# Second edge loop of a four-layer graph kernel: joining maximum and denominator in PSUM with VectorE and ScalarE instead of TensorE, and 36 instead of 32 of 125 gathered columns a turn by TensorE

## The chip, the cores and the metric

One core of one Trainium2 chip runs the whole program. The metric is the time on the device in microseconds (us), the median of several runs. The engines are called TensorE (PE in the profile; PEld are its weight loads), VectorE (DVE), ScalarE (ACT), GpSimd (POOL) and SyncE (SP).

## The reference, cut to what matters

Node features x (12,500 nodes of 32 features) go through four layers, each of which adds to x what it makes of `h = relu(layernorm(x))` over 400,000 edges sorted by receiver. The second layer, the one that is changed, is attention over the edges:

```python
scores = jnp.sum(Q[receiver] * K[sender], axis=1) * scale
smax = jax.ops.segment_max(scores, receiver, num_segments=n)
alpha = jnp.exp(scores - smax[receiver])
Z = jax.ops.segment_sum(alpha, receiver, num_segments=n)
alpha = alpha / (Z[receiver] + 1e-06)
out = jax.ops.segment_sum(alpha[:, None] * V[sender], receiver, num_segments=n)
return x + out @ Wo
```

## The kernel before, in words

The edges are cut into 125 chunks (`NCH`) of 4 groups by 800 edges (`CH`), walked in 25 turns (`TURNS`) of 5 chunks (`RING`). There is one edge loop for each layer, and between the loops a short stage over the nodes. In a chunk's tile, `rows`, each of 128 partitions holds 25 edges (columns) of 32 features. A column is filled with the senders' features in one of two ways.

**By GpSimd**: an indirect DMA (L492) fetches the rows of one column from the table in memory; behind each stands a memset of a tile called `pace` (L497), whose end the engine waits for.

**By TensorE**: `gather_tile` multiplies a one-hot matrix with the node table held in SBUF (`h_parts`): 14 matmuls at L690, in the second loop behind one more, L686, that adds a far value to the rows of the wrong blocks. The block's one-hot row `h0_hot` is made by VectorE in `make_h0_hot` (L904), for the next chunk but one, inside `turn_mz`. VectorE then reduces the tile from PSUM into the column (`pick`, L912). `PE_COLS[1]` says how many columns of each of the five chunks go this way: (7, 7, 6, 6, 6), so 32 of 125, 6.4 a chunk. GpSimd does the other 93. In this loop the tiles have two PSUM banks (`TILE_BUFS[1]` is 2), so that a tile is begun only when VectorE has picked the last but one. The one-hot matrices are cast by ScalarE (L546) from tiles that a DMA brings back (L554), four tiles ahead.

**The order by hand in the second loop**: While VectorE works through chunk r (`attend`, then `turn_in` of chunk r+1, then `turn_mz` of chunk r), TensorE makes the tiles of chunk r+1. In `attend` VectorE scans the queries (L1179) and multiplies them with the keys (L1180); it picks tiles 0 and 1; TensorE sums the products over the features into `acc_wide` (L738: the scores); VectorE scans the running maximum (L1187, with L1185 ahead), subtracts it from the scores (L1190) and picks tiles 2 and 3. Meanwhile ScalarE makes from that difference the decay and the weight by two Relus (L626, L627) and two Exps (L629, L631). Then come the scan of the denominator Z (L1195), the product (L1197), the scan of the messages (L1198), a small copy (L1199), the transpose of the messages out (L1201), and the picks from tile 4 on. `turn_in` transposes the next chunk's rows (L1163) and queries (L1165). `turn_mz` makes the block one-hot (L904) and transposes `acc_wide` out (L1210). On TensorE the tiles 0 and 1 come first, then the scores, the other tiles, and at the end of each chunk 12 matmuls (L745), which write into `acc_wide` the new maximum for the lower half of the features and Z for the upper half: the sum of three products with constant 0/1 matrices (`mz_parts`, loaded by SyncE from `c_mz`). TensorE must have the one-hot row of the next chunk before that chunk's tile 0.

Of the kernel before, what the change touches and what calls it, by code (L numbers as in the profile page):

```python
# [38 lines left out]
ALU = mybir.AluOpType  # L39
# [3 lines left out]
P = 128  # L43
# [14 lines left out]

PE_COLS = ((8, 8, 8, 8, 8), (7, 7, 6, 6, 6), (8, 8, 8, 8, 8), (6, 6, 5, 5, 6))
PACE = 288  # L60
# [17 lines left out]
def gnn_kernel(nc, x_in, src_c, src_pe, dst_c, dst_p, dst_blocks, pattern_c, sh_c, wq, wk, wv, wo, w2, w3,  # L78
               c_ones, c_tri, c_group, c_iota, c_half, c_diag, c_sel, c_expand, c_mz, c_coupling, c_target, c_shift, out):
    KT = x_in.shape[1]  # L80
# [30 lines left out]
    with ExitStack() as ctx:  # L111
# [51 lines left out]
        nb_wide = work[:, 12:14, :].rearrange("p a c -> p (a c)")[:, 0:CH + 1]  # L163
        mz_parts = qh[:, 0:3 * P].rearrange("p (a m) -> p a m", m=P)
        h0_width = max(PE_COLS[1]) * P // 2
# [79 lines left out]
        window_loaded, keep_made, keep_stored = sem("window_loaded"), sem("keep_made"), sem("keep_stored")  # L245
        prod_ready, score_ready, z_ready, mz_made, mz_loaded, nb_ready = sem("prod_ready"), sem("score_ready"), sem("z_ready"), sem("mz_made"), sem("mz_loaded"), sem("nb_ready")
        decay_in, decay_ready, p_in, p_ready = sem("decay_in"), sem("decay_ready"), sem("p_in"), sem("p_ready")
# [109 lines left out]
        def _(sp):  # L357
# [40 lines left out]
            for l in range(LAYERS):  # L398
# [6 lines left out]
                if l == 3:  # L405
                    sp.wait_ge(sh_stored, 32 * NCH + START)
                if l == 1:
                    sp.dma_start(mz_parts.rearrange("p a m -> p (a m)"), c_mz).then_inc(mz_loaded, 16)
                with sp.Fori(0, TURNS) as t:
# [105 lines left out]
        def _(act):  # L515
# [100 lines left out]
            with act.Fori(0, TURNS) as t:  # L616
                for r in range(RING):
# [12 lines left out]
                    act.wait_ge(decay_in, n)  # L630
                    nc.scalar.activation(u, u, ACT.Exp, scale=-1.0).then_inc(decay_ready, 1)  # L631
                    cast_next(1, t, r, range(2, PE_MAX))
                    store(1, t, r, attn_chunks, 2 * CH)
# [30 lines left out]
        def _(pe):  # L664
# [64 lines left out]
            gather_first(1)  # L729
            pe.wait_ge(mz_loaded, 16)  # L730
            with pe.Fori(0, TURNS) as t:
                for r in range(RING):
                    for i in tiles(1, r + 1, range(2)):
                        gather_tile(1, t, i, per_turn[1])
                    pe.wait_ge(prod_ready, chunk_no(0, t, r))
                    pe.wait_ge(outs_ready[(r - 1) % RING], use(1, t, 0 if r else -1))
                    for cols in SPANS:
                        last = nc.tensor.matmul(acc_wide[:, cols], group_ones[:, :], prod[:, cols], start=True, stop=True)  # L738
                    last.then_inc(score_ready, 1)
                    for i in tiles(1, r + 1, range(2, PE_MAX)):  # L740
                        gather_tile(1, t, i, per_turn[1])
                    pe.wait_ge(z_ready, chunk_no(0, t, r))
                    for cols in SPANS:
                        for part, rows_in in enumerate((prod, d, Z)):
                            last = nc.tensor.matmul(acc_wide[:, cols], mz_parts[:, part, :], rows_in[:, cols],  # L745
                                                    start=(part == 0), stop=(part == 2))
                    last.then_inc(mz_made, 1)
            for q in range(PIECES):
# [44 lines left out]
        def _(v):  # L793
# [361 lines left out]
            steps1 = steps[0]  # L1155
            per_chunk1 = 5

# [10 lines left out]
            def attend(t, r):  # L1168
# [24 lines left out]
                v.wait_ge(decay_ready, n)  # L1193
                v.wait_ge(p_ready, n)
                nc.vector.tensor_tensor_scan(Z, u, in_ps, last_of(Z), ALU.mult, ALU.add).then_inc(z_ready, 1)  # L1195
                v.wait_ge(z_ready, n)
# [3 lines left out]
                v.wait_ge(outs_stored[r], t * 16 + (1 * TURNS * 16 + START))  # L1200
                then(nc.vector.transpose(row[:, :, 0:D], by_edge(in_ps)))  # L1201
                pick_next(1, t, r, range(4, PE_MAX))
                assert at[0] == per_chunk1

            def turn_mz(t, r):

                make_h0_hot(t, r + 2)
                v.wait_ge(mz_made, chunk_no(0, t, r))
                row = outs[:, r, :].rearrange("p (j f) -> p j f", j=J)
# [214 lines left out]
def constants(KT):  # L1424
# [23 lines left out]
    for k, (n, i) in enumerate(LAYER3_TERMS):  # L1448
# [12 lines left out]
        else:  # L1461
# [18 lines left out]
        "c_expand": (np.arange(mul)[:, None] == inner[None]).astype(np.float32),  # L1480
        "c_mz": np.stack([(group[:, None] == group[None]) & (feature[None] < D // 2),
                          np.eye(P, dtype=bool) & (feature[None] < D // 2),
                          np.eye(P, dtype=bool) & (feature[None] >= D // 2)], axis=1).astype(np.float32).reshape(P, 3 * P),
        "c_coupling": coupling,
# [5 lines left out]
_INS = ("x_in", "src_c", "src_pe", "dst_c", "dst_p", "dst_blocks", "pattern_c", "sh_c", "wq", "wk", "wv", "wo", "w2", "w3",  # L1490
        "c_ones", "c_tri", "c_group", "c_iota", "c_half", "c_diag", "c_sel", "c_expand", "c_mz", "c_coupling", "c_target", "c_shift")

# [46 lines left out]
```

## Time and profile before

| | |
|---|---|
| median of 3 runs | 15984.19 us (15972.8 to 16000.97) |
| profiled execution, first to last instruction (span) | 14816.7 us |
| between that span and the median of the runs | 1167.5 us |
| second edge loop, from its first to its last transposed chunk (L1163) | 3801.3 to 7276.4 us |
| TensorE, VectorE, ScalarE, GpSimd busy over the span | 87%, 65%, 26%, 84% |

The profile gives the span of its execution and no time of its own for what lies around it, so the table sets the span against the median. A row of the timeline gives start, duration, engine, line, operation, output and input, how many instructions were merged, and in brackets how long the engine had been idle and who ended it. A row of groups gives count, busy time, the mean of one, and the idle time ahead. "Clock" is TensorE's granted clock as a share of 2.4 GHz.

### The profile page before, as it was taken

To read this page: it belongs to the slowest core of one execution; us is meant where nothing else is said; L and a number is where in the kernel's file an instruction comes from. 1 tells how busy PE (TensorE), PEld (TensorE's weight loads), DVE (VectorE), ACT (ScalarE), POOL (GpSimd) and SP (SyncE) were. 2 spreads that over 40 slices of the span, in tenths; PEclk is the share of its full clock that TensorE was granted. 3 is DMA by queue.
4 is the path that set the end of the run, shared out by engine and by line. 5 is a ranking of instruction groups with operands and counts; after the bars stand their busy time and mean duration, and the time that the engine had idled before them with its cause. 6 is when DMAs were issued, how large, how long until landed. Compare 5 with 4: busy or idle time off the path is not lost.

```text
span 14816.7 us, 226154 instructions
## 1 busy us (share of the span) xinstructions
PE 12890.3 (87%) x57644; PEld 10677.8 (72%) x57644; DVE 9612.6 (65%) x13223; ACT 3874.6 (26%) x4265; POOL 12431.7 (84%) x18594
## 2 busy tenths in 40 slices
PE   7999999992699999999689999999769999999996
PEld 6888888881577777777578888888756666767764
DVE  7666666664577777777666666666656665666665
ACT  2222222220233333333222222222211111111111
POOL 6888888887888888888778888888888888888884
PEclk9999999995899999999889999999989999999998
DMA  5444444442344444444345555545433333333332
GB/s 174 148 148 157 157 155 151 149 151 46 101 123 122 124 124 123 122 123 124 90 119 130 129 130 128 131 127 131 110 76 87 86 90 83 90 86 87 87 86 56
DMA packets 1340717, 1727.48 MB, mean 117 GB/s; under 512 B 501932, under 2 KB 1145566, under 8 KB 1339646
## 3 DMA queue, kind: packets, MB, share of 16 engines
q10 hardware_dynamic: 705956, 1154.87, 24.6%
q1 hardware_dynamic: 327194, 407.86, 9.6%
q0 software_dynamic: 306880, 158.96, 7.6%
q14 instruction: 668, 5.47, 0.1%
q8 instruction: 19, 0.31, 0.0%
HBM read 1140.23 MB, written 580.36 MB: 116 GB/s over the span
## 4 chain that ended last, share of the span: by engine, by line
POOL 41%; issue 32%; PE 20%; DVE 5%; POOLq 1%; DMA 0%; DVEq 0%; ACT 0%; ACTq 0%; SPq 0%
POOL rows L492 22%; POOL pace L497 16%; PE psum L690 12%; PE psum L773 7%; POOL outs L509 2%; PE psum L764 2%; DVE work L1340 1%; DVE work L1315 1%; POOLq L496 1%; POOL q_edges L471 1%; POOL work L501 1%; DVE tile_rows L924 0%; DVE work L1323 0%; DVE rows L931 0%; DVE outs L1347 0%
## 5 line engine op out<-in xcount | busy, mean ns | idle before, releaser
L690 PE MATMUL psum<-h_parts,one_hot 128*128 128x448 f32 x49406 | 10813.2, 377 | 482.0 <-ACT one_hot L539 262.4
L690 PEld LDWEIGHTS psum<-h_parts,one_hot 128*128 128x128 f32 x49406 | 9428.8, 192 | 1500.6 <-ACT one_hot L539 313.0
L492 POOL DMA_INDIRECT rows<-h_table,idx x9000 | 8662.9, 963 | 1966.9 <-POOL pace L497 1537.1
L546 ACT ACTIVATE one_hot<-keys 128x896 fp32r<-128x896 bf16 x2533 | 2359.9, 950 | 6435.5 <-PE psum L690 4314.0
L497 POOL MEMSET pace<- 128x288 f32 x9000 | 3213.9, 357 | 18.1 <-issue 13.2
L924 DVE TENSOR_TENSOR tile_rows<-psum,h_mask 128x448 f32<-128x448 f32 x2722 | 1686.2, 619 | 1252.3 <-PE psum L690 991.3
L931 DVE TENSOR_REDUCE rows<-tile_rows 128x32 f32<-128x448 f32 x2722 | 1677.0, 616 | 58.9
L773 PE MATMUL psum<-work,bd_t 128*128 128x512 f32 (+1 forms) x3500 | 1359.2, 514 | 240.1 <-DVE work L1323 141.3
L1323 DVE TENSOR_TENSOR work<-psum,work 128x800 f32<-128x800 f32 x875 | 862.7, 988 | 920.9 <-PE psum L764 864.2
L773 PEld LDWEIGHTS psum<-work,bd_t 128*128 128x128 f32 x3500 | 654.9, 193 | 764.4 <-issue 443.4
L912 DVE TENSOR_REDUCE rows<-psum 128x32 f32<-128x448 f32 x807 | 503.1, 623 | 792.0 <-PE psum L690 741.7
L539 ACT ACTIVATE one_hot<-work 128x896 fp32r<-128x896 bf16 x506 | 482.0, 953 | 1493.3 <-DVE work L887 1493.3
L539 ACT ACTIVATE one_hot<-bit_hot 128x896 fp32r<-128x896 bf16 x506 | 482.6, 954 | 883.4 <-DVE bit_hot L887 880.5
L1028 DVE STREAM_TRANSPOSE psum<-rows 128x800 f32<-128x800 f32 x125 | 128.2, 1026 | 864.0 <-DMA rows<-h_table,idx 864.0
L686 PE MATMUL psum<-work 128*128 128x448 bf16 x807 | 296.3, 367 | 308.0 <-DVE work L904 223.6
L745 PE MATMUL psum<-work 128*128 128x512 f32 x1500 | 524.1, 499 | 0.0
L509 POOL DMA_INDIRECT outs<-sums,end_row x294 | 291.6, 992 | 258.3 <-DMA sums<-outs 147.0
L686 PEld LDWEIGHTS psum<-work 128*128 128x128 bf16 x807 | 78.2, 97 | 501.6 <-DVE work L904 276.3
L745 PEld LDWEIGHTS psum<-work 128*128 128x128 f32 x1500 | 284.2, 189 | 210.3 <-issue 179.8
L764 PE MATMUL psum<-work,sel 120*128 120x512 bf16 x1750 | 427.4, 337 | 0.0
L1163 DVE STREAM_TRANSPOSE work<-rows 128x800 f32<-128x800 f32 x125 | 213.7, 1710 | 207.7 <-DMA rows<-h_table,idx 188.4
L1293 DVE STREAM_TRANSPOSE psum<-rows 128x800 f32<-128x800 f32 x125 | 128.2, 1026 | 289.7 <-DMA rows<-h_table,idx 289.7
(202 smaller groups left out, 6198.1 us busy)
## 6 DMA issues: line engine op xcount, KB each, us to landing
keys<-hots ACTq DMA_DIRECT2D x2542, 224.0 KB
keep_in<-keep_flat SPq DMA_DIRECT2D x2000, 100.0 KB
sums<-outs ACTq DMA_DIRECT2D x375, 400.0 KB
rows<-h_table,idx POOLq DMA_INDIRECT x9000
hots<-bit_hot ACTq DMA_DIRECT2D x506, 224.0 KB
hots<-work ACTq DMA_DIRECT2D x506, 224.0 KB
attn<-outs ACTq DMA_DIRECT2D x125, 800.0 KB
edge_in<-pattern_c SPq DMA_DIRECT2D x125, 400.0 KB
```

Of the source, the lines that this page charges most:

```text
L492: nc.gpsimd.indirect_dma_start(out=rows[:, r, j * D:(j + 1) * D], out_offset=None, in_=h_table[:, :], in_offset=bass.IndirectOffsetOnAxis( ...
L497: nc.gpsimd.memset(pace[:, :], 0.0).then_inc(pause_ended, 1)
L509: nc.gpsimd.indirect_dma_start(out=node_rows[:, k * width:(k + 1) * width], out_offset=None, in_=table[:, :], in_offset=bass.IndirectOffse ...
L539: nc.scalar.activation(one_hots[i % LOOK[l]][:, :, :], bit_hots[i % BIT_BUFS[l]], ACT.Copy).then_inc(one_hot_cast, 1)
L546: nc.scalar.activation(one_hots[i % LOOK[l]][:, :, :], loaded_hots[i % BIT_BUFS[l]], ACT.Copy).then_inc(one_hot_cast, 1)
L690: last = nc.tensor.matmul(banks[TILE_BANKS[l][b]][:, 0:H0 * D], one_hots[hot][:, h1, :], h_parts[:, part, h1 * H0 * D:(h1 + 1) * H0 * D], ...
L745: last = nc.tensor.matmul(acc_wide[:, cols], mz_parts[:, part, :], rows_in[:, cols], start=(part == 0), stop=(part == 2))
L764: last = nc.tensor.matmul(bcast[n % 2][:, cols], sel[0:SH_ROWS, n, :], shT[r][:, cols], start=True, stop=True)
L773: last = nc.tensor.matmul(acc_wide[:, cols], bd_t[:, n, :], weighted[n % 4][:, cols], start=(n == 0), stop=(n == PRODUCTS - 1))
L924: nc.vector.tensor_tensor(tile_rows[:, :].rearrange("p (f h) -> p f h", f=D), banks[TILE_BANKS[l][b]][:, 0:H0 * D].rearrange("p (f h) -> p ...
L931: nc.vector.reduce_sum(rows[:, chunk % RING, j * D:(j + 1) * D], tile_rows[:, :].rearrange("p (f h) -> p f h", f=D), axis=AX_X).then_inc(p ...
L1323: nc.vector.tensor_tensor(weighted[n % 4], bcast[n % 2], hT, ALU.mult).then_inc(weighted_ready, 1)
```

## The change

Two things change in the second edge loop. First, the 12 matmuls at the end of a chunk go, with their constant and its load. In their place VectorE makes, ahead of the scan of Z, `max(acc_wide, 0) + mx` in place (the difference to the old maximum, cut at zero, plus the old maximum); ScalarE multiplies it with a 0/1 mask for the lower half of the features, behind its two Exps; and after the transpose of the messages VectorE adds Z times the mask for the upper half. Second, the columns by TensorE become (7, 7, 7, 7, 8), 36 of 125, which leaves 89 to GpSimd.

```diff
-PE_COLS = ((8, 8, 8, 8, 8), (7, 7, 6, 6, 6), (8, 8, 8, 8, 8), (6, 6, 5, 5, 6))
+PE_COLS = ((8, 8, 8, 8, 8), (7, 7, 7, 7, 8), (8, 8, 8, 8, 8), (6, 6, 5, 5, 6))
...
-        mz_parts = qh[:, 0:3 * P].rearrange("p (a m) -> p a m", m=P)
...
-                if l == 1:
-                    sp.dma_start(mz_parts.rearrange("p a m -> p (a m)"), c_mz).then_inc(mz_loaded, 16)
...
                     nc.scalar.activation(u, u, ACT.Exp, scale=-1.0).then_inc(decay_ready, 1)
+                    act.wait_ge(m_made, n)
+                    nc.scalar.activation(acc_wide, acc_wide, ACT.Copy, scale=half[:, 0:1]).then_inc(m_masked, 1)
                     cast_next(1, t, r, range(2, PE_MAX))
...
             gather_first(1)
-            pe.wait_ge(mz_loaded, 16)
...
                     for i in tiles(1, r + 1, range(2, PE_MAX)):
                         gather_tile(1, t, i, per_turn[1])
-                    pe.wait_ge(z_ready, chunk_no(0, t, r))
-                    for cols in SPANS:
-                        for part, rows_in in enumerate((prod, d, Z)):
-                            last = nc.tensor.matmul(acc_wide[:, cols], mz_parts[:, part, :], rows_in[:, cols],
-                                                    start=(part == 0), stop=(part == 2))
-                    last.then_inc(mz_made, 1)
...
-            per_chunk1 = 5
+            per_chunk1 = 6
...
                 v.wait_ge(p_ready, n)
+                nc.vector.scalar_tensor_tensor(out=acc_wide, in0=acc_wide, scalar=0.0, in1=mx[:, 0:CH],
+                                               op0=ALU.max, op1=ALU.add).then_inc(m_made, 1)
                 nc.vector.tensor_tensor_scan(Z, u, in_ps, last_of(Z), ALU.mult, ALU.add).then_inc(z_ready, 1)
...
                 then(nc.vector.transpose(row[:, :, 0:D], by_edge(in_ps)))
+                v.wait_ge(m_masked, n)
+                then(nc.vector.scalar_tensor_tensor(out=acc_wide, in0=Z, scalar=half[:, 1:2], in1=acc_wide,
+                                                    op0=ALU.mult, op1=ALU.add))
                 pick_next(1, t, r, range(4, PE_MAX))
...
                 make_h0_hot(t, r + 2)
-                v.wait_ge(mz_made, chunk_no(0, t, r))
```

The input `c_mz` goes from the argument list and from `constants`.

## Rows read from the trace of the kernel before

**Rows 1.** Stretches: second loop, one turn; length, PE PEld DVE ACT POOL, clock, DMA, GB/s.

```profile
3801.30:7307.00 3505.70, 3195.92 (x13960) 2553.84 (x13961) 2475.95 (x2548) 1252.48 (x1446) 3015.30 (x4614) 0.98 0.43 122
5503.00:5643.10 140.10, 128.76 (x561) 102.71 (x561) 98.98 (x103) 50.25 (x59) 121.60 (x187) 0.98 0.44 123
```

**Rows 2.** The chain of waits, 5500 to 5560 us, shares by line.

```profile
by line: issue 42.0%; POOL rows L492 32.8%; POOL pace L497 24.8%; POOLq L496 1.1%; POOLq L490 0.1%; POOLq L495 0.1%
```

**Rows 3.** Groups on GpSimd, second loop.

```profile
L492 POOL DMA_INDIRECT rows<-h_table,idx x2307 | 2194.6, 951 | 457.7 <-POOL pace L497 399.2 <-issue 58.5
L497 POOL MEMSET pace<- 128x288 f32 x2307 | 828.0, 359 | 1.2
```

**Rows 4.** Line L1163 over the run, and its entry among the loop's waits.

```profile
L1163 DVE STREAM_TRANSPOSE work<-rows x125: 1661/1712/1770, 3801.3 to 7276.4; 128x800 f32<-128x800 f32 x125
DVE work L1163 <- DMA rows<-h_table,idx: 188.4, 61, 112.0
```

**Rows 5.** Timeline of VectorE from 5495 us.

```profile
5495.97 1.88 DVE L1187 TENSOR_TENSOR_SCAN mx<-psum,mx,work 128x800 f32<-128x800 f32 x1 [0.28 <-PE psum L738]
...
5502.02 0.62 DVE L912 TENSOR_REDUCE rows<-psum 128x32 f32<-128x448 f32 x1 [2.45 <-PE psum L690]
5502.87 1.88 DVE L1195 TENSOR_TENSOR_SCAN work<-work,psum 128x800 f32<-128x800 f32 x1 [0.23 <-DVE rows L912]
...
5508.98 0.62 DVE L912 TENSOR_REDUCE rows<-psum 128x32 f32<-128x448 f32 x1
...
5513.03 0.62 DVE L912 TENSOR_REDUCE rows<-psum 128x32 f32<-128x448 f32 x1 [2.57 <-PE psum L690]
...
5516.78 0.41 DVE L904 TENSOR_SCALAR work<-work,half 14x768 bf16<-14x768 int16 x1 [0.15 <-DVE psum L1165]
...
5524.95 1.88 DVE L1187 TENSOR_TENSOR_SCAN mx<-psum,mx,work 128x800 f32<-128x800 f32 x1 [0.29 <-PE psum L738]
...
5552.26 1.88 DVE L1187 TENSOR_TENSOR_SCAN mx<-psum,mx,work 128x800 f32<-128x800 f32 x1 [0.29 <-PE psum L738]
...
5577.90 1.88 DVE L1187 TENSOR_TENSOR_SCAN mx<-psum,mx,work 128x800 f32<-128x800 f32 x1 [0.29 <-PE psum L738]
```

**Rows 6.** Timeline of TensorE over the end of the same chunk.

```profile
5509.76 0.35 PE L686 MATMUL psum<-work 128*128 128x448 bf16 x1 [1.70 <-DVE rows L912]
5509.78 3.21 PE L690 MATMUL psum<-h_parts,one_hot 128*128 128x448 f32 x14
5512.83 4.20 PE L745 MATMUL psum<-work 128*128 128x512 f32 x12
5517.24 0.36 PE L686 MATMUL psum<-work 128*128 128x448 bf16 x1 [0.21 <-DVE work L904]
```

**Rows 7.** Groups of VectorE and ScalarE: the nearest kin of the new instructions.

```profile
L1197 DVE TENSOR_TENSOR psum<-psum,work 128x800 f32<-128x800 f32 x125 | 124.9, 999 | 4.3
L844 DVE SCALAR_TENSOR_TENSOR work<-work,ln 128x448 f32<-128x448 f32 x28 | 17.5, 625 | 0.9
L836 DVE TENSOR_TENSOR work<-xs,ln 128x448 f32<-128x448 f32 x7 | 4.4, 624 | 0.2
L626 ACT ACTIVATE work<-psum 128x800 f32<-128x800 f32 x125 | 104.8, 839 | 535.7 <-DVE psum L1190 535.7
```

**Rows 8.** TensorE's tiles behind long pauses: first, one exception, last of thirteen.

```profile
4728.43 0.55 PE L686 MATMUL psum<-work 128*128 128x448 bf16 x1 [3.71 <-DVE work L904]
4728.48 4.74 PE L690 MATMUL psum<-h_parts,one_hot 128*128 128x448 f32 x14
...
7000.22 3.20 PE L690 MATMUL psum<-h_parts,one_hot 128*128 128x448 f32 x14
...
7279.59 5.67 PE L690 MATMUL psum<-h_parts,one_hot 128*128 128x448 f32 x14
```

**Rows 9.** Windows inside a tile behind a 4.81 us pause, and inside a usual tile.

```profile
5317.60:5319.60 2.00, 2.00 (x6) 1.79 (x7) 1.97 (x2) 0.11 (x1) 1.83 (x4) 0.50 0.18 59
5502.00:5504.80 2.80, 2.80 (x15) 2.46 (x14) 2.52 (x3) 1.69 (x3) 2.47 (x5) 1.00 0.52 133
```

More of the change, by code:

```diff
@@ L78, in gnn_kernel @@
 def gnn_kernel(nc, x_in, src_c, src_pe, dst_c, dst_p, dst_blocks, pattern_c, sh_c, wq, wk, wv, wo, w2, w3,
-               c_ones, c_tri, c_group, c_iota, c_half, c_diag, c_sel, c_expand, c_mz, c_coupling, c_target, c_shift, out):
+               c_ones, c_tri, c_group, c_iota, c_half, c_diag, c_sel, c_expand, c_coupling, c_target, c_shift, out):
     KT = x_in.shape[1]
@@ L245, in gnn_kernel @@
         window_loaded, keep_made, keep_stored = sem("window_loaded"), sem("keep_made"), sem("keep_stored")
-        prod_ready, score_ready, z_ready, mz_made, mz_loaded, nb_ready = sem("prod_ready"), sem("score_ready"), sem("z_ready"), sem("mz_made"), sem("mz_loaded"), sem("nb_ready")
+        prod_ready, score_ready, z_ready, m_made, m_masked, nb_ready = sem("prod_ready"), sem("score_ready"), sem("z_ready"), sem("m_made"), sem("m_masked"), sem("nb_ready")
         decay_in, decay_ready, p_in, p_ready = sem("decay_in"), sem("decay_ready"), sem("p_in"), sem("p_ready")
@@ L1480, in constants @@
         "c_expand": (np.arange(mul)[:, None] == inner[None]).astype(np.float32),
-        "c_mz": np.stack([(group[:, None] == group[None]) & (feature[None] < D // 2),
-                          np.eye(P, dtype=bool) & (feature[None] < D // 2),
-                          np.eye(P, dtype=bool) & (feature[None] >= D // 2)], axis=1).astype(np.float32).reshape(P, 3 * P),
         "c_coupling": coupling,
@@ L1490 @@
 _INS = ("x_in", "src_c", "src_pe", "dst_c", "dst_p", "dst_blocks", "pattern_c", "sh_c", "wq", "wk", "wv", "wo", "w2", "w3",
-        "c_ones", "c_tri", "c_group", "c_iota", "c_half", "c_diag", "c_sel", "c_expand", "c_mz", "c_coupling", "c_target", "c_shift")
+        "c_ones", "c_tri", "c_group", "c_iota", "c_half", "c_diag", "c_sel", "c_expand", "c_coupling", "c_target", "c_shift")
 def laid_out(a):
```

## The prediction

> **What bounds the kernel now.** The change touches one loop of four, so I read in this order: the stretch of that loop, its chain of waits, the groups of the engine that the chain names, and then the timelines of VectorE and TensorE over one chunk.
>
> The stretches [rows 1] show TensorE busy for 128.8 of the 140.1 us of a turn, GpSimd for 121.6, VectorE for 99.0, ScalarE for 50.3. TensorE looks like the bound. The chain of waits says otherwise [rows 2]: it is GpSimd's gathers, its pace memsets and its own issue, nothing else. A column costs GpSimd the gather's 0.951 us, the memset's 0.359 and idle time between them of 457.7/2307 = 0.198 with what stands at the start of a chunk [rows 3]: 1.508 us in all, and 93 x 1.508 = 140.2 us is the turn. The loop's chunks are (7276.4 - 3801.3)/124 = 28.02 us apart [rows 4], 140.1 a turn, 3,503 us for 125.
>
> How far is the second chain behind? VectorE waited 188.4 us for gathered rows, 112.0 of them once, before the first chunk [rows 4]. That leaves 76.4 us over 124 chunks, 0.6 a chunk. So the chain of VectorE and TensorE is only about 3 us a turn shorter than GpSimd's, and whatever lengthens it by more decides. I therefore follow it step by step.
>
> In the timeline of VectorE [rows 5] the maximum scan (L1187) of one chunk stands at 5495.97 and the next at 5524.95: 28.98 us for a chunk in which TensorE makes seven tiles and no gathered row is late. From 5552.26 to 5577.90, with six tiles, it is 25.64. The order inside: pick of tile 3 at 5502.02, scan of Z, product, scan, transpose, pick of tile 4 at 5508.98, of tile 6 at 5513.03, block one-hot at 5516.78, the next maximum. In the timeline of TensorE [rows 6] tile 6 starts at 5509.76, after a pause of 1.70 us that ends with the pick of tile 4: there are two banks, and tile 6 needs tile 4's. The 12 matmuls take 4.20 us at 5512.83, and the next tile 0 starts at 5517.24, after 0.21 us, when the one-hot row is made. So those 12 matmuls lie inside the time in which TensorE has to wait for VectorE's L904 in any case. That is the main reading.
>
> **The change, part by part.**
>
> *The 12 matmuls go.* TensorE is free 4.2 us earlier and then waits for L904: nothing is gained on the chain. In a six-tile chunk it is the same. Their constant's load happens once, beside other work: 0.
>
> *Two sums on VectorE.* Each is 128x800 in fp32 with one input in PSUM. A tensor-tensor of that size and kind takes 0.999 us (L1197); at 128x448 the same operation as the new one takes 0.625 against 0.624 of a tensor-tensor [rows 7]. So 1.0 each, 1.03 with the step's wait. Bounds: 0.6 each (the 448-wide row), and the 1.88 of a scan [rows 5], which also does two operations per element; the equal 448-wide rows speak for 1.0. Both stand on VectorE between the pick of tile 3 and that of tile 4, behind which are queued the remaining picks, the transposes and L904, and TensorE waits for pick 4 and for L904. So all of it is on the chain: +2.06 us a chunk.
>
> *The mask on ScalarE*: an Activate of 128x800 from PSUM, 0.84 us (L626) [rows 7]. It starts behind the first sum and must be done at the second; between them lie the scan of Z, the product, the scan, the copy and the transpose, 5508.98 - 5502.87 = 6.1 us [rows 5]. Hidden. It holds back the one-hot casts behind it on ScalarE by up to 2 us; these run four tiles ahead, and tile 6 is wanted only after pick 4, some 9 us after pick 3. Cost 0; without that cover it would be 0.84 + 1.0. Between 0 and 1 us a chunk, I take 0.
>
> *Columns.* GpSimd: 89 x 1.508 = 134.2 us a turn, 5.9 less. TensorE and VectorE: four chunks of 7 tiles and one of 8. An eighth tile follows the seventh at once (its bank is free), so it adds one tile: 5512.83 - 5509.76 = 3.07 us [rows 6].
>
> *The chain at full clock*: 4 x (28.98 + 2.06) + (28.98 + 2.06 + 3.07) = 124.2 + 34.1 = 158.3 us a turn, against GpSimd's 134.2. The bound moves, and the turn grows by 18.2 us. GpSimd will run ahead and stand idle at `rows_used`.
>
> *TensorE's pauses.* They grow: before tile 6 from 1.70 to 1.70 + 2.06 = 3.8 us, before the next tile 0 from 0.21 to 5517.24 - 5509.78 - 3.21 = 4.25 us [rows 6]. What does such a pause do? In the loop before there are thirteen pauses of 3.6 to 4.8 us ahead of a tile, from 4728.4 to 7279.6 us [rows 8]. Behind one (at 7000.2, pause 3.77) the tile takes the usual 3.23 us; behind the other twelve it takes 4.4 to 5.7, mean of all thirteen 4.80. The stretch inside such a tile shows a granted clock of 0.50, that is 1.2 GHz, against 1.00, 2.4 GHz, in a usual one [rows 9]. Pauses such as the one of 1.70 us [rows 6], some sixty of 1.6 to 1.8, never did this; those of 2.3 to 3.1 did in about half the cases. So each pause costs 4.80 - 3.23 = 1.57 us, and both kinds lie on the chain: VectorE waits for tile 6 and, for the scores, for tiles 0 and 1. Ten pauses a turn: +15.7 us. Bounds: 0, and 2.4 (the longest tile, from 4.16 us) each, 24.
>
> The Trainium skill has this as a rule, page "TensorE: Matmul & The Clock Gate", section "HAM oscillation — how this bites in real kernels": a kernel whose bursts of matmuls are parted by waits loses the full clock in each wait and starts each burst cold. By that rule all ten pauses would cost, with no exception like the one at 7000.2; the trace agrees in twelve of thirteen.
>
> *Sum*: 158.3 + 15.7 = 174.0 us a turn, x 25 = 4,350, against 3,503: +847 us. On the execution shown the span goes from 14,816.7 to 15,664. I take the 1,167.5 us between span and median as unchanged and get 15,984 + 847 = 16,831. The other three loops have the same instructions.
>
> **The rivals.**
>
> *Full clock in most pauses.* For it: the exception at 7000.2, and that the clock was mixed behind pauses not much shorter. Against: twelve of thirteen. 158.3 x 25 = 3,958, +455 us: 16,439.
>
> *GpSimd stays the bound, the kernel gets faster.* The mechanism: VectorE's sums and picks fit into its present waits for tiles (it is busy only 99 of 140 us), so the turn is GpSimd's 134.2 us: -147 us, 15,837. It decides where the other chain is under 134.2 a turn, 26.8 a chunk. For it: TensorE has 12 x 0.35 = 4.2 us a chunk less and one tile in 1.25 chunks more, 2.5 us. Against: the 28.98 us of a seven-tile chunk before, which has no wait for rows in it and whose order is not changed. If some reordering gained just the difference, it would be no change; I see none.
>
> *The clock stays low for longer.* With two colder tiles a chunk TensorE is busy for some 27 of 35 us instead of 25.7 of 28. If tiles 1 and 2 and the scores were slow too, with about 1.5 us more for each of two of them on the chain: 125 x 3 = +375 on top, 17,206. The rows show the second tile at full speed after each such pause, so this is unlikely.
>
> *The change doesn't do what it says* (the columns not moved, the sums alone): then turns of 3 x (25.64 + 2.06) + 2 x 31.04 = 145.2, plus seven or eight pauses of 1.57, 157: +420 us, 16,400. The `PE_COLS` line is plain, so I count this with the first rival.
>
> **How the numbers follow.** Forecast 0.73; full clock in most pauses 0.12; clock low for longer 0.08; GpSimd the bound 0.05; nothing measurable 0.02. The range leaves out the ends: its lower end is half of the pauses at full clock with something to spare (3,958 + 5 x 25 x 1.57 = 4,154, +651, less the sums at 0.6 instead of 1.03, -108: 16,527, I take 16,560), its upper end all ten pauses at 2.0 us (4,458, +955: 16,939), with 50 us for the wider L904 and the mask: 16,990. A measurement of this kernel can tell about 0.2%, 32 us, from no change. Slower 0.93, same 0.02, faster 0.05.
>
> **What would show it right or wrong.** Right: the new sums at 1.0 us each; L1163 every 34 to 35 us; GpSimd no longer gapless, waiting for VectorE; VectorE no longer waiting for DMA at L1163; TensorE with pauses of 3.8 us before tile 6 (released by L912) and 4.2 before tile 0 (released by L904), and tiles of 4.7 us or so behind them; a granted clock near 0.9 in the loop instead of 0.98. Wrong: gathers of GpSimd still gapless; VectorE's seven-tile chunk under 30 us; pauses without the slow tile behind them; a Z scan or second sum that waits for ScalarE.

## The result, and the profile after

| | before | after |
|---|---|---|
| median of the runs compared | 15,989.9 us (4 runs) | 16,517.0 us (4 runs, 16,456.8 to 16,519.8) |
| ratio | | 1.0317, 95% interval 1.0298 to 1.0335 |
| span of the profiled execution | 14,816.7 us | 16,454.3 us |
| second edge loop, first to last chunk | 3,475 us, 28.02 a chunk | 4,472 us, 36.06 a chunk |

The change makes the kernel slower by 527 us. The forecast was 847 us, and the measured time lies 43 us under the low end of the range.

To read the numbers one must know that the same program did not take the same time in each comparison, that is, in each session in which kernels were timed side by side. The kernel before, unchanged, had these medians: 15,990 us in the first comparison (the one of the table), 14,809 in the second, 16,204 in the third, 15,276 in the fourth and 16,028 in the fifth. Within one comparison most of its executions lie within 0.6% of the median. The results carry a chip number: 10 for the second comparison, 14 for the third, 15 for the fourth and 10 again for the fifth; the first has none. So the chip's number does not explain the difference: 14,809 and 16,028 us both stand beside number 10. The text speaks of the conditions of a comparison, and means no more by it than this time of the kernel before. A few single executions took far longer at a much lower granted clock (19,577 us at 0.62 in one case, against 15,281) and are left out of every ratio.

The profile ahead of the prediction has a span of 14,816.7 us, close to the 14,809 of the second comparison, while the runs that it was set against took 15,990. So the two spans and the two second loops in the table must not be compared with each other. The two medians can be.

The page of the kernel after: busy time, then the chain that ended last.

```profile
PE 13401.3 (81%) x57644; PEld 11054.5 (67%) x57644; DVE 9894.6 (60%) x13573; ACT 4089.1 (25%) x4490; POOL 12308.6 (75%) x18394
...
PE 49%; issue 20%; DVE 14%; POOL 11%; another core or an unknown queue 4%; ACT 1%; ACTq 1%; DVEq 0%; POOLq 0%; DMA 0%; SPq 0%
```

GpSimd is no longer most of the chain. The groups of the second loop, kernel after: GpSimd's gathers, the picks, a tile's first matmul, the two sums and the mask.

```profile
L489 POOL DMA_INDIRECT rows<-h_table,idx x2203 | 2100.1, 953 | 1441.0 <-DMA idx<-src_c 1070.8 <-issue 214.7 <-POOL pace L494 155.5
...
L904 DVE TENSOR_REDUCE rows<-psum 128x32 f32<-128x448 f32 x893 | 557.9, 625 | 1524.5 <-PE psum L689 1160.5 <-issue 275.8 <-remote 55.8
L685 PE MATMUL psum<-work 128*128 128x448 bf16 x891 | 367.2, 412 | 1043.3 <-DVE work L896 487.9 <-DVE rows L904 270.7 <-issue 238.4
...
L1197 DVE SCALAR_TENSOR_TENSOR psum<-work,half,psum 128x800 f32<-128x800 f32 x124 | 130.9, 1056 | 4.4
L1187 DVE SCALAR_TENSOR_TENSOR psum<-psum,mx 128x800 f32<-128x800 f32 x124 | 124.0, 1000 | 28.4 <-issue 19.9 <-DVE rows L904 8.5
L630 ACT ACTIVATE psum<-psum,half 128x800 f32<-128x800 f32 x124 | 111.9, 902 | 313.2 <-DVE psum L1187 277.4 <-issue 35.9
```

Against [rows 3], where GpSimd stood idle for 458 us, mostly behind its own pace memset, it now waits 1,071 us for the column indices, which SyncE loads only when VectorE has given the rows' buffer free. TensorE stands idle for 1,043 us ahead of a tile's first matmul: 488 for L896 (the block one-hot, L904 before), 271 for picks (L904, L912 before) and 238 put down to issue, which is time for which the profile shows no cause. The same group in the loop of the kernel before had 304 us:

```profile
L686 PE MATMUL psum<-work 128*128 128x448 bf16 x798 | 292.9, 367 | 303.9 <-DVE work L904 219.4 <-DVE rows L912 83.7
```

The sums take 1.00 and 1.06 us, with no wait ahead of the second. Over the second loop the granted clock is 0.85, against 0.98 in [rows 1] (length, PE PEld DVE ACT POOL, clock, DMA, GB/s):

```profile
3827.00:8299.00 4472.00, 3423.65 (x13871) 2869.74 (x13869) 2751.93 (x2877) 1444.93 (x1662) 2879.69 (x4407) 0.85 0.36 100
```

The timeline of TensorE in the kernel after, one chunk, answers to [rows 6]:

```profile
6057.77 3.19 PE L689 MATMUL psum<-h_parts,one_hot 128*128 128x448 f32 x14
6064.61 0.53 PE L685 MATMUL psum<-work 128*128 128x448 bf16 x1 [3.65 <-DVE rows L904]
6064.63 5.64 PE L689 MATMUL psum<-h_parts,one_hot 128*128 128x448 f32 x14
6074.26 0.56 PE L685 MATMUL psum<-work 128*128 128x448 bf16 x1 [3.99 <-DVE work L896]
6074.31 5.73 PE L689 MATMUL psum<-h_parts,one_hot 128*128 128x448 f32 x14
```

Here is the mechanism that was forecast: a pause of 3.65 us before tile 6 and of 3.99 before the next tile 0, each followed by a tile of 5.6 to 5.8 us instead of 3.2. A tile that is slow in this way, at about half the granted clock, is called cold below.

### The profile page after: what moved, and what is told of

Same layout as the page of the kernel before. It is cut to its first block, busy times and chain, and to the rows that moved or that the text cites. A ratio compares the mean times of both kernels' runs of the same rounds, so it can differ in the third digit from the quotient of the medians.

```text
span 16454.3 us, 227519 instructions
## 1 busy us (share of the span) xinstructions
PE 13401.3 (81%) x57644; PEld 11054.5 (67%) x57644; DVE 9894.6 (60%) x13573; ACT 4089.1 (25%) x4490; POOL 12308.6 (75%) x18394
## 4 chain that ended last, share of the span: by engine, by line
PE 49%; issue 20%; DVE 14%; POOL 11%; another core or an unknown queue 4%; ACT 1%; ACTq 1%; DVEq 0%; POOLq 0%; DMA 0%; SPq 0%
PE psum L689 39%; POOL rows L489 6%; PE psum L765 6%; POOL pace L494 5%; PE psum L756 2%; DVE tile_rows L916 1%; PE psum L685 1%; DVE rows L904 1%; PE psum L736 1%; DVE work L1336 1%; DVE psum L1157 1%; DVE work L1189 1%; ACT one_hot L543 1%; DVE work L1311 1%
## 5 line engine op out<-in xcount | busy, mean ns | idle before, releaser
L689 PE MATMUL psum<-h_parts,one_hot 128*128 128x448 f32 x50806 | 11788.5, 390 | 708.9 <-issue 308.5
L689 PEld LDWEIGHTS psum<-h_parts,one_hot 128*128 128x128 f32 x50806 | 10081.3, 200 | 2011.8 <-issue 838.9
L489 POOL DMA_INDIRECT rows<-h_table,idx x8900 | 8574.8, 963 | 3481.6 <-DMA idx<-src_c 1685.6
L543 ACT ACTIVATE one_hot<-keys 128x896 fp32r<-128x896 bf16 x2633 | 2455.2, 949 | 7764.5 <-PE psum L689 3219.3
L904 DVE TENSOR_REDUCE rows<-psum 128x32 f32<-128x448 f32 x907 | 566.7, 625 | 1648.6 <-PE psum L689 1177.4
L685 PE MATMUL psum<-work 128*128 128x448 bf16 x907 | 374.0, 412 | 1151.0 <-DVE work L896 505.5
L1020 DVE STREAM_TRANSPOSE psum<-rows 128x800 f32<-128x800 f32 x125 | 128.1, 1025 | 619.1 <-DMA rows<-h_table,idx 619.1
L879 DVE TENSOR_TENSOR bit_hot<-keys,target 128x896 bf16<-128x896 int16 x506 | 310.4, 614 | 0.0
L879 DVE TENSOR_TENSOR work<-keys,target 128x896 bf16<-128x896 int16 x506 | 309.6, 612 | 0.0
L756 PEld LDWEIGHTS psum<-work,sel 120*128 120x128 bf16 x1750 | 175.5, 100 | 177.3 <-issue 13.3
L506 POOL DMA_INDIRECT outs<-attn,end_row x98 | 94.6, 966 | 218.2 <-DMA attn<-outs 188.6
```

Of the source, the lines that this page charges most:

```text
L489: nc.gpsimd.indirect_dma_start(out=rows[:, r, j * D:(j + 1) * D], out_offset=None, in_=h_table[:, :], in_offset=bass.IndirectOffsetOnAxis( ...
L543: nc.scalar.activation(one_hots[i % LOOK[l]][:, :, :], loaded_hots[i % BIT_BUFS[l]], ACT.Copy).then_inc(one_hot_cast, 1)
L685: nc.tensor.matmul(banks[TILE_BANKS[l][b]][:, 0:H0 * D], h0_hots[H0_BUF[chunk % RING]][:, q * P:(q + 1) * P], far, start=True, stop=False)
L689: last = nc.tensor.matmul(banks[TILE_BANKS[l][b]][:, 0:H0 * D], one_hots[hot][:, h1, :], h_parts[:, part, h1 * H0 * D:(h1 + 1) * H0 * D], ...
L756: last = nc.tensor.matmul(bcast[n % 2][:, cols], sel[0:SH_ROWS, n, :], shT[r][:, cols], start=True, stop=True)
L904: nc.vector.reduce_max(rows[:, chunk % RING, j * D:(j + 1) * D], banks[TILE_BANKS[l][b]][:, 0:H0 * D].rearrange("p (f h) -> p f h", f=D), ...
```

## The experiments

All times are medians; each ratio is to the kernel before in the same comparison. A loop's length comes from the one profiled execution of a run, and is the time between the first and last of its 125 transposes, so of 124 chunks.

**Second comparison (the kernel before: 14,809 us).** Was the first profile an unusual execution? `e0_before_again` is the kernel before, unchanged.

> The kernel before, unchanged, profiled again. Theory A (the first profiled execution, 14,817 us, was unusually fast; what lay between its span and the median of 15,990 is not fixed time around the program but slower edge loops): span near 15,980, second loop about 32 us a chunk instead of 28.0, loops three and four some 350 and 170 us longer than in that profile, as in the profile of the changed kernel. Rival B (a fixed time around the span): span 14,800 to 14,850, second loop 28.0 us a chunk.

Measured: 14,807.4 us, ratio 0.9999 (0.9990 to 1.0009), span 14,802.2, second loop 28.01. Neither expectation was right as it stood. Span and loop are those of rival B, but its reason falls: the run with that span took 14,804.0 us, so there is no 1,167 us around the span. The first profile is a usual execution under the conditions of the second comparison; what differs are the conditions.

`e1_sums_only` is the changed kernel with the old columns:

```diff
-PE_COLS = ((8, 8, 8, 8, 8), (7, 7, 7, 7, 8), ...
+PE_COLS = ((8, 8, 8, 8, 8), (7, 7, 6, 6, 6), ...
```

> The changed kernel with the old columns (7, 7, 6, 6, 6): only the two sums and the mask. Theory A (VectorE's chain takes the 2.06 us of the sums, and TensorE's longer pauses make the tile behind them cold): three six-tile chunks of 27.7 and two of 31.0, with some eight cold tiles of 1.6 to 2.5 us: 31.5 to 33 us a chunk in the second loop, 16,000 to 16,250 in all if the rest is as in the changed kernel. Rival C (the sums cost nothing, the columns do it): no slower than before, 15,990 or less.

`e2_columns_only` is the kernel before with the new columns, the same line the other way.

> The kernel before with the new columns (7, 7, 7, 7, 8): TensorE keeps the 12 matmuls. Theory A: seven-tile chunks of 29.0 us and one of 32.0, no pause ahead of tile 0 beyond 0.2 us, so hardly a cold tile: 29.5 to 30.5 us a chunk, 16,050 to 16,300 if GpSimd was the bound in the timed runs too, and about 15,700 to 15,990 if those runs' second loop stood at 32 us for another reason. Rival C (columns by TensorE are what costs): 16,400 or more.

Measured: e1 15,083.1 us, ratio 1.0183 (1.0166 to 1.0200); e2 14,829.2, ratio 1.0014 (1.0004 to 1.0024). The transposes of the second loop, e1 and then e2, and those of the fourth loop, e0 and then e2:

```profile
L1157 DVE STREAM_TRANSPOSE psum<-edge_in x125: 1032/1057/1082, 3796.9 to 7697.4; 128x800 f32<-128x800 f32 x125
```

```profile
L1165 DVE STREAM_TRANSPOSE psum<-edge_in x125: 1034/1065/1104, 3798.8 to 7454.2; 128x800 f32<-128x800 f32 x125
L1347 DVE STREAM_TRANSPOSE outs<-work x125: 1667/1732/1799, 11088.1 to 14689.5; 128x800 f32<-128x800 f32 x125
```

```profile
L1347 DVE STREAM_TRANSPOSE outs<-work x125: 1671/1730/1799, 10903.6 to 14663.8; 128x800 f32<-128x800 f32 x125
```

The second loop takes 3,900.5/124 = 31.46 us a chunk with the sums alone and 3,655.4/124 = 29.48 with the columns alone. The prediction's arithmetic gives 157/5 = 31.4 for the first, and 4 x 28.98 + 28.98 + 3.07 = 148.0, so 29.6 a chunk, for the second. Both parts cost, the sums 3.5 us a chunk and the columns 1.5, and rival C falls. Both loops lie a few hundredths of a microsecond under the expected 31.5 to 33 and 29.5 to 30.5. The expected totals (16,000 to 16,250, and 15,700 or more) missed by about 900 us, since they were built on the first comparison's times. Both parts together, the changed kernel itself, were not run in this comparison. But e2 is only 20 us slower in all, though its second loop is 182 us longer: the fourth loop, whose code is the same, takes 3,601 us instead of 3,760. In e1 it takes 3,618.

`e3_early_pick_and_row` does the changed kernel's work in another order on VectorE:

```diff
                 then(nc.vector.tensor_tensor(in_ps, in_ps, hT, ALU.mult))
+                pick_next(1, t, r, range(4, 5))
                 then(nc.vector.tensor_tensor_scan(in_ps, u, in_ps, o_last, ALU.mult, ALU.add))
                 nc.vector.tensor_copy(o_last, last_of(in_ps))
+                pick_next(1, t, r, range(5, 6))
+                make_h0_hot(t, r + 2)
...
-                pick_next(1, t, r, range(4, PE_MAX))
+                pick_next(1, t, r, range(6, PE_MAX))
...
             def turn_mz(t, r):
-                make_h0_hot(t, r + 2)
```

> The changed kernel with the same work in another order on VectorE: the picks of tiles 4 and 5 right behind the product and the message scan, and the block one-hot behind them, so that TensorE waits neither before tile 6 nor before the next tile 0. Theory A (the chain with its pauses is the loss): the pauses of about 3.8 and 4.2 us shrink under 1 us, the granted clock goes back over 0.95, the second loop falls from 36.1 to 27 to 29 us a chunk, time 15,400 to 15,700. Rival D (something that does not hang on the pauses, such as instruction supply on TensorE or the DMAs, sets the loop): 16,400 or more.

Measured: 14,711.4 us, ratio 0.9934 (0.9914 to 0.9954), second loop 28.47 us a chunk. The changed kernel's sums and columns, with all their work, now take 0.5 us a chunk more than the kernel before in the same comparison; the prediction had put them at 6.8. No tile in this loop stands behind a pause of over 1 us, though 37 are still cold, behind the scores. So the loss is in the pauses. The expected total of 15,400 to 15,700 was again built on the first comparison and says nothing here; the fourth loop takes 3,600 us here too.

**Third comparison (16,204 us).** `e7_after_again` is the changed kernel, unchanged; `e4_early_pick` has only the picks of e3's diff, `e5_early_row` only the moved `make_h0_hot`.

> The changed kernel, unchanged, on whichever chip comes, beside the kernel before. In the first comparison the kernel before took 15,990 us, in the second 14,809. Theory A (both loops' lengths are as the chain of VectorE and TensorE gives them): where the kernel before takes 14,810, the second loop takes 34 to 36 us a chunk, 750 to 1,000 us more than before, and the fourth loop, which took 3,760 us in the kernel before and 3,600 in all three variants of it, gives 150 back: 15,400 to 15,650. Rival B (the change costs what the first comparison shows, wherever it runs): ratio 1.03, 15,280.

> The changed kernel with the picks of tiles 4 and 5 behind the product and the message scan, the block one-hot left in its place. Theory A: the pause before tile 6 goes, with the cold tile behind it (3.8 + about 2 us of each chunk, of which VectorE's own work hides some); the pause before tile 0 grows: second loop 31 to 33 us a chunk. Rival (only the pause before tile 0 matters): hardly shorter than the changed kernel's.

> The changed kernel with the block one-hot made behind the message scan, the picks left in their place. Theory A: tile 0 follows the last tile of the chunk before without a pause, and its work lies beside VectorE's transposes: some 4 us and the cold tile less a chunk, second loop 29.5 to 32 us a chunk; the pause before tile 6 and its cold tile stay. Rival (only the pause before tile 6 matters): 34 us or more.

Measured: e7 16,630.5 us, ratio 1.0265 (1.0229 to 1.0300), second loop 36.09. e4 16,160.2, ratio 0.9971 (0.9945 to 0.9997), 32.48 a chunk. e5 16,206.5, ratio 1.0005 (0.9983 to 1.0027), 32.49. Each of the two moves alone is worth 3.6 us a chunk, and either gives back the whole 426 us of loss (470 and 424 us). In e4 the pause before tile 6 is gone, and that before tile 0 is 6.4 us instead of 4.2, with all 123 tiles behind it cold; in e5 there is no pause before tile 0, and that before tile 6 stays. e5's 32.49 is just above its expected 29.5 to 32. e7's second loop is as long as in the first comparison, 4,475 against 4,472 us, while the kernel before takes 214 us more: the ratio depends on the conditions. e7's 1.0265 is near what its rival B said; the fourth comparison gives another ratio.

`e6_before_early` is the kernel before with both reorderings.

> The kernel before with both reorderings and its own columns. Theory A: GpSimd's 93 columns a turn bound it at 28.0 us a chunk whatever VectorE does, so the second loop stays at 28.0; the time changes by less than 50 us apart from the fourth loop, which may give 150 back as in the other variants. Rival (VectorE's chain bounds the kernel before too): 27 us or less a chunk, 100 us gained in the second loop.

Measured: 15,990.2 us, ratio 0.9865 (0.9827 to 0.9903), second loop 31.03 us a chunk, so neither 28.0 nor 27. Under these conditions something else than GpSimd's 28.0 sets the loop even with both moves, which led to the next question.

**Fourth comparison (15,276 us).** `e8_before_third` and `e9_after_third` are both kernels, unchanged.

> The kernel before, unchanged, a third time. So far chips gave it 15,990, 14,809 and 16,204 us, and its two profiles are both of executions near 14,810. If this chip is of the slower kind, theory A (TensorE's queue is late with instructions there, which shows as idle time put down to issue, and the kernel before has no slack on TensorE to hide it): second loop 31 to 33 us a chunk instead of 28.0, TensorE's idle time put down to issue several times that of the first profile. Rival B (the slower kind of chip loses its time outside the second loop): second loop 28 us a chunk. If the chip is of the faster kind, the run only repeats the first: 14,810.

> The changed kernel, unchanged, a third time. On a chip of the faster kind, theory A gives 34 to 36 us a chunk in the second loop, hardly less than the 36.1 of the slower kind, since TensorE stands idle for 8 us of each chunk and hides late instructions there: 15,450 to 15,700 in all, ratio 1.045 to 1.06. On the slower kind: again 36.1 us a chunk and ratio 1.025 to 1.035.

Measured: e8 15,280.8 us, ratio 1.0007; its profiled execution has a span of 19,574 us, so it says nothing on the second loop. e9 15,928.5 us, ratio 1.0434 (1.0415 to 1.0452), second loop 35.38 us a chunk. Over that loop 247 pauses of more than 3.4 us stand ahead of a tile, and behind every one of them the tile takes over 4.2 us; the mean of the 247 is 5.08 with the opening matmul, against 3.21 for the 644 tiles with no pause. The loop is in the 34 to 36 expected for faster conditions, the ratio just under their 1.045.

`e10_filler` puts matmuls whose result is overwritten into the pause before tile 0:

```diff
                     if q == 0:
+                        for _ in range(18):
+                            nc.tensor.matmul(banks[TILE_BANKS[l][b]][:, 0:H0 * D], one_hots[hot][:, 0, :],
+                                             h_parts[:, 0, 0:H0 * D], start=True, stop=True)
                         pe.wait_ge(h0_hot_made, h0_made(c, chunk))
```

> The changed kernel with 18 more matmuls ahead of each chunk's tile 0, between the wait for the free bank and the wait for the block one-hot; what they write is overwritten. They fill about 3.7 of the 4.2 us pause with work that serves nothing. Theory A (the pause costs by the clock: the tile behind it runs at 1.2 GHz): tile 0 takes 3.2 us again instead of 4.4 to 5.8, and the second loop gets 1.3 to 2.3 us a chunk shorter, 160 to 290 us in all, though TensorE does more. Rival E (the clock costs nothing on the chain, the longer tile is hidden): no change, or slower by what the matmuls overlap with the chain.

Measured: 15,719.0 us, ratio 1.0297 (1.0279 to 1.0315), second loop 33.69. The timeline of TensorE in e10, from the pause that is left to the tile behind the filler:

```profile
5512.43 0.53 PE L688 MATMUL psum<-work 128*128 128x448 bf16 x1 [3.65 <-DVE rows L907]
5512.45 5.73 PE L692 MATMUL psum<-h_parts,one_hot 128*128 128x448 f32 x14
5517.98 4.01 PE L685 MATMUL psum<-h_parts,one_hot 128*128 128x448 f32 x18
5522.28 0.36 PE L688 MATMUL psum<-work 128*128 128x448 bf16 x1 [0.29 <-DVE work L899]
5522.32 3.13 PE L692 MATMUL psum<-h_parts,one_hot 128*128 128x448 f32 x14
```

Tile 6 behind its pause is still cold (5.73; over the loop, 116 of 124), tile 0 behind the filler takes 3.1 to 3.2, and none of the 124 is cold. More work on TensorE makes the kernel 209 us faster than the changed one, 1.69 us a chunk: the clock's share of that pause, and rival E falls. It also shows what the 12 matmuls of the kernel before can do beside their sum. In e2, which has them and where VectorE's chain sets the pace, the pause before tile 0 is 0.2 us in the mean and no tile 0 is cold. In the kernel before itself that held in part only: in the first profile 74 of 124 tiles 0 stand behind a pause of over 1 us, and 40 are cold, which costs little where GpSimd is the bound.

`e11_scores_later` is e3, with tile 2 ahead of the scores on TensorE and the pick of tile 0 ahead of the query scan:

```diff
-                    for i in tiles(1, r + 1, range(2)):
+                    for i in tiles(1, r + 1, range(3)):
...
-                    for i in tiles(1, r + 1, range(2, PE_MAX)):
+                    for i in tiles(1, r + 1, range(3, PE_MAX)):
...
+                pick_next(1, t, r, range(1))
                 v.wait_ge(keep_loaded[r], use(1, t) * (16 * G))
...
-                pick_next(1, t, r, range(2))
+                pick_next(1, t, r, range(1, 2))
```

> The variant with early picks and early one-hot row, and beside them tile 2 moved ahead of the scores on TensorE, the pick of tile 0 ahead of the query scan on VectorE. In that variant on the faster chip (28.47 us a chunk) TensorE waits 3.2 to 4.1 us for the product ahead of the scores, and the scores and the tile behind them then run cold. Theory A: that pause shrinks under 1.2 us, the second loop falls to GpSimd's bound of 26.8 to 27.3 us a chunk on a faster chip, 0.5 to 1.5 us less a chunk than the variant without it on a slower one. Rival F (VectorE's own work, 22 us a chunk and its waits, is the bound by now): no gain.

Measured: 14,997.1 us, ratio 0.9821 (0.9803 to 0.9838), second loop 27.91 us a chunk. It beats both kernels of this comparison. The loop is shorter than e3's 28.47 of the second comparison, but not at GpSimd's 26.8; e3 was not run here, so the worth of the later scores alone is not shown.

**Fifth comparison (16,028 us).** `e12_before_fourth` and `e13_after_fourth` are both kernels once more, `e14_40_columns` is e11 with (8, 8, 8, 8, 8).

> The kernel before, unchanged. Theory A: on a chip where it takes over 15,200 us its second loop is longer than the 28.0 us a chunk of the two profiles near 14,810 (29 to 32), with more of TensorE's idle time put down to issue, and part of the change's loss is thereby already paid. Rival B: the second loop is 28.0 there too and the other loops alone are longer. On a chip with 14,810 it only repeats the first profile.

> The changed kernel, unchanged. On a chip where the kernel before takes 14,810 us, theory A gives 34.5 to 35.4 us a chunk in the second loop (35.4 and 36.1 were seen at 15,276 and 15,990 to 16,204), 15,500 to 15,700 in all if the fourth loop takes 3,600 us as in the other variants, ratio 1.047 to 1.06. On a slower chip: 35.4 to 36.1 and ratio 1.025 to 1.045.

> The variant with early picks, early one-hot row and later scores, with 40 of 125 columns by TensorE instead of 36. GpSimd's 85 columns would bound it at 25.6 us a chunk, TensorE's 8 tiles and scores at 26.0. Theory A (TensorE is now close to the bound, any pause or late instruction adds): 27.5 to 29 us a chunk, no better than with 36. Rival G (GpSimd still bounds the variant with 36): 1.1 us less a chunk, 140 us less in all.

Measured: e12 16,043.2 us, ratio 0.9999 (0.9985 to 1.0012); e13 16,495.7, ratio 1.0285 (1.0268 to 1.0302); e14 15,759.1, ratio 0.9839 (0.9822 to 0.9856), 29.91 a chunk, which is above the 27.5 to 29 of theory A. The gain is the same as e11's within the intervals: four more columns by TensorE bring nothing that can be seen, and rival G falls, as far as two comparisons with different conditions can tell. The transposes of the second and of the fourth loop, e12 and then e13:

```profile
L1165 DVE STREAM_TRANSPOSE psum<-edge_in x125: 1031/1059/1117, 3896.4 to 7816.2; 128x800 f32<-128x800 f32 x125
L1347 DVE STREAM_TRANSPOSE outs<-work x125: 1666/1722/1779, 11933.5 to 16063.8; 128x800 f32<-128x800 f32 x125
```

```profile
L1157 DVE STREAM_TRANSPOSE psum<-edge_in x125: 1037/1062/1085, 3920.0 to 8383.9; 128x800 f32<-128x800 f32 x125
L1343 DVE STREAM_TRANSPOSE outs<-work x125: 1660/1721/1792, 12500.7 to 16496.8; 128x800 f32<-128x800 f32 x125
```

In one comparison, then, the second loop goes from 3,920 to 4,464 us (31.61 to 36.00 a chunk, +544), the fourth from 4,130 to 3,996 (-134); the first and third differ by 32 and 8. The spans, 16,202.8 and 16,636.4, differ by 434; each belongs to an execution about 1% above its run's median, and the medians differ by 453. What holds the kernel before up in its second loop there: its longest waits between 3,950 and 7,800 us in e12.

```profile
ACT one_hot L546 <- remote: 751.7, 262, 6.4
ACT work L622 <- issue: 603.1, 98, 8.7
DVE rows L912 <- PE psum L690: 565.3, 271, 6.0
PEld psum L686 <- issue: 555.5, 560, 8.8
ACT one_hot L546 <- PE psum L690: 525.7, 259, 6.6
DVE rows L912 <- remote: 455.0, 152, 6.2
POOL rows L492 <- DMA idx<-src_c: 386.7, 61, 13.2
```

TensorE's weight load at the head of a tile waits 556 us for issue (110 in the loop of the first profile), VectorE's picks wait 455 us for a releaser that the profile doesn't know (none there), and GpSimd waits 387 us for indices. VectorE's transpose L1163 no longer waits for gathered rows at all, against 188 us in [rows 4]. So in e12 the chain of TensorE and VectorE is the bound already. With the longer pauses come cold tiles: 126 of them, 40 in the first profile. A pick in the timeline of e12 shows how:

```profile
5528.12 4.51 PE L690 MATMUL psum<-h_parts,one_hot 128*128 128x448 f32 x14
5532.47 4.20 PE L745 MATMUL psum<-work 128*128 128x512 f32 x12
5534.53 0.62 DVE L912 TENSOR_REDUCE rows<-psum 128x32 f32<-128x448 f32 x1 [5.30 <-remote]
```

The tile's last matmul is recorded as ended at 5,532.63, and the pick starts 1.90 us later; in [rows 5, 6] it is 5,513.03 against 5,512.99, 0.04. This is no single case: of the 491 picks of this loop that waited for over 0.3 us, 148 start over 1.5 us behind the recorded end of the tile before them (median 0.80), while in e0 none of 330 does (median 0.04). In the changed kernel of the same comparison, e13, it is 22 of 592 (median 0.04). The profile models the ends of matmuls, so this tells that the signal is late, not why.

## Why the prediction was wrong in size

**What bounded the kernel before.** GpSimd's 28.0 us a chunk is right for the conditions of the profile (28.01 again in e0). It is not right for those under which both kernels were compared: e12, where the kernel before takes 16,028 us, close to the 15,990 of the first comparison, has 31.61. This is the step that failed: "I take the 1,167.5 us between span and median as unchanged", and with it the 3,503 us for the old second loop in the sum. The difference was no fixed time around the program but slower loops, the second among them by some 3.6 us a chunk. For the first comparison itself this is inferred, since the kernel before has no profile from it; in the fifth both kernels have one, and the gap between their second loops is 4.4 us a chunk instead of the 6.8 of the forecast. A gap of 7% between a profile and its runs should have been read as a sign that they are not of the same conditions, and GpSimd's bound, only 3 us a turn ahead of the other chain, as one that such conditions would overturn.

**The 12 matmuls: nothing gained.** Right, and the reason was half of it: they lay inside a wait, and they can keep the clock up (e2, e10).

**The sums, +2.06.** Right: 1.00 + 1.06. **The mask, 0.** Right: the second sum has no wait but the 0.04 of the step.

**The pauses.** Right in place and length: forecast 3.8 us before tile 6 and 4.25 before tile 0, in e9 the means are 3.9 and 4.1. Each was priced at 1.57 us; e9 shows 5.08 - 3.21 = 1.87, so 18.7 a turn instead of 15.7, 0.6 a chunk. With it the forecast of 34.8 becomes 35.4, which is e9's 35.38; that the two agree so closely is in part luck, as e9's conditions are not those of the profile. The first, third and fifth comparisons have 36.0 to 36.1; that the 0.7 above are of the same kind as what holds up e12 is not shown. Two counts of the prediction were loose: of pauses of 2.3 to 3.1 us in the old loop, 25 of 35 had a cold tile behind them and not half, and over the whole loop there are fourteen of 3.6 us or more, thirteen of them with a cold tile. The rule of the Trainium skill, page "TensorE: Matmul & The Clock Gate", section "HAM oscillation — how this bites in real kernels", that each burst behind a wait starts cold, holds for 247 of 247 pauses of over 3.4 us in e9, and for 116 of 124 in e10.

**GpSimd's bound goes; it waits for VectorE.** Right: 1,071 us for indices.

**"The other three loops have the same instructions"**, so the same time: wrong by -134 us in the fifth comparison, for the fourth loop.

**The range.** Its low end was worked out as 16,527 and then taken as 16,560; the measured 16,517 is under both. No term in it stood for a kernel before whose own loop is longer.

The sum for the first comparison then: second loop (36.0 - 31.6) x 125 = +550 instead of +847, fourth loop -134, the first and third +40, about +456. Measured were 527 there and 434 between the profiled executions of the fifth comparison, so some 70 us of the first stay unexplained. The change's size is not one number. The ratio is 1.0434 where the kernel before takes 15,276 us, 1.0317 at 15,990, 1.0285 at 16,028 and 1.0265 at 16,204. Where it was profiled, the old second loop went from 28.0 to 31.6 us a chunk between faster and slower conditions and the new one only from 35.4 to 36.1, so the slower the conditions, the more of the loss the kernel before has already paid. That the changed kernel hides late signals in TensorE's idle time would fit, and no run tests it. The changed kernel has not been run where the kernel before takes 14,809 us; the forecast's own case is untested.

## What to carry to other kernels

A matmul inside a forced wait is not only free, it can be what keeps TensorE's clock up; before moving it to another engine, count the pauses that it leaves and what stands behind them. Where two banks and one consumer set the pace, look at the order of that consumer's work first: moving two picks (e4) or one small one-hot (e5) gave back the whole 2.65% of loss in the third comparison, and with both moves and the later scores the kernel is 1.8% faster than before (e11). The old kernel gains from both moves too (1.35%, e6); old and new sums with the same order were not set against each other in one comparison. And check that a profile and the runs it is set against are of the same conditions before a bound with a margin of 2% is built on it.

## What the runs showed of the hardware that was not expected

**The same program took 14,809 to 16,204 us in different comparisons**, each repeatable within it, and 14,809 and 16,028 us under the same chip number. The profiles put the extra time to late releases by TensorE and to issue. It is not that more instructions were loaded: the DMA queue that the profile calls "instruction" (q14) moved 127 packets during the second loop both in e0 and in e12. What causes it was not found, and no run isolates it.

**The fourth loop depends on the code ahead of it.** Its instructions are the same in e0 and e2. The waits of VectorE in that loop (11,100 to 14,600 us) that are put down to issue, e0 and then e2:

```profile
DVE h_mask L896 <- issue: 76.3, 22, 4.1
DVE tile_rows L924 <- issue: 72.6, 29, 3.8
```

```profile
DVE tile_rows L924 <- issue: 2.0, 10, 0.2
DVE h_mask L896 <- issue: 0.5, 1, 0.5
```

The 146 us that vanish, about 6 a turn, are nearly the 159 by which the loop gets shorter. VectorE stands there for nothing that the profile shows, once or twice a turn. One count in the traces goes with it: during the fourth loop the instruction queue q14 moved 265 packets in e0 and 126 in e2, with 150 in e1 (3,618 us) and 127 in e3 (3,600 us); in the fifth comparison it was 265 in e12 (4,130 us) and 127 in e13 (3,996 us). More packets alone don't lengthen every loop, though: in the third loop e0 has 125 and e3 365, at 3,154 and 3,159 us. That VectorE's instructions come late at the loop's turn, depending on where the code lies, fits all of this, but no run changes that alone. It is 1% of the kernel, as much as many a change is meant to bring, and it made e2 look harmless.
